# Causal mask of a 16-head attention: by TensorE into PSUM, or by VectorE on negated scores

## The chip, the cores and the metric

The program runs on one core of one Trainium2 chip. The core has a matrix engine (TensorE), two engines for elementwise work on 128 partitions (VectorE and ScalarE), a programmable one (GpSimd), and SyncE, which issues most transfers. Each engine runs its own instructions in order, and they wait for one another through semaphores. TensorE writes to PSUM, the accumulator memory; VectorE and ScalarE read PSUM and SBUF, GpSimd only SBUF. The metric is the device time of one execution in microseconds, and lower is better.

## The reference

Eight layers work on a state `x` of 32 sequences of 128 tokens of width 128, all float32: attention, linear experts, wide attention, capacity experts, attention with selection, GELU experts, attention, quantised convolution. Only the third, the wide attention, is touched. Cut to what matters it is

```python
# q = layernorm(x), k = v = ctx_1024; 16 heads of width 64; w_q, w_k, w_v are 1024 x 128
qh = (q @ w_q.T).reshape(b, n, H, D_K).transpose(0, 2, 1, 3)      # kh, vh likewise
scores = jnp.einsum('bhid,bhjd->bhij', qh, kh) / math.sqrt(D_K)
causal = jnp.tril(jnp.ones((n, n), dtype=bool))
scores = jnp.where(causal[None, None], scores, -jnp.inf)
attn = jax.nn.softmax(scores, axis=-1)
out = jnp.einsum('bhij,bhjd->bhid', attn, vh)
out = out.transpose(0, 2, 1, 3).reshape(b, n, H * D_V)
x = x + jnp.tanh(g_xattn[1]) * (out @ w_o.T)
```

So each query may look at keys up to its own place, and the others get probability 0.

## The kernel before

`program` keeps `x` in SBUF for the whole run and calls the stages one after another, each in a block of its own, so that a stage starts when every engine is through with the one before it. `setup` writes constants: among them, by GpSimd, `causal` (0 up to the diagonal and -1e30 above it, 128x128 in bf16) and `causal_swapped`, the same table with its halves of 64 rows exchanged.

`attention_wide` (from L2106) goes over 64 steps n. A step is one sequence and one octet of heads: 8 heads, so that 2 steps make a sequence and 4 steps a group of two sequences. `scores[n % 2]` is a PSUM tile of 1024 columns, two halves h of 4 heads (c) by 128 keys. Within a step:

- TensorE, `score(n)` (L2217): four bf16 matmuls of 64 rows by 64 columns of the array and 512 moving columns write the mask into the two halves (L2227). They use the four quadrants of the array, one each. Then 8 float32 matmuls of 64 rows add q times k on top of it (L2232); the trace has two records for each float32 matmul.
- VectorE, `maximum(n)` (L2375): one reduction over the 1024 columns gives 8 negated maxima.
- ScalarE, `exponents(n, h)` (L2315): four exponentials of 128 columns for each half, with the negated maximum as bias, and the row sums beside them. q was scaled as it was copied out of PSUM (L2304).
- VectorE, `invert(n, h)` (L2383): reciprocals of the four row sums of a half.
- GpSimd (L2183): the probabilities of a half times these reciprocals, in SBUF.
- TensorE, `turn(n)` (L2264): 16 transposes of 64 columns put the probabilities back into `scores[n % 2]`, turned. The second half waits for GpSimd's second product.
- VectorE, `copy_turned(n, h)` (L2368): two copies of 512 columns to SBUF. `score(n + 2)` waits for both.
- TensorE, `contexts(n)` (L2238), ScalarE, `context_copy(n)` (L2308), TensorE, `project_out(n)` (L2252): probabilities times v, their copy, and the output product. VectorE then adds the result to `x` once for each sequence (L2394) and takes its statistics (L2399).

The inputs of the next group are made between these by TensorE, `make(f)` (L2191): 13 tiles for each group, x, k0 to k3, q0 to q3, v0 to v3, into two PSUM buffers in turn. `make(f)` waits until tile f - 2 has been copied out. x and the q's are copied by ScalarE, the k's and v's by VectorE (`keep`, L2353). The 13 tiles are dealt to the four steps of a group: four, three, three and three (`quarter`, L2140).

The order on each engine is written out by hand. TensorE, in step n: the first two tiles of the step, `score(n + 1)`, `turn(n)`, `contexts(n - 1)`, the other tiles, `project_out(n - 1)`. ScalarE: copies of the first two tiles, `context_copy(n - 1)`, `exponents(n + 1, 0)`, the other copies, `exponents(n + 1, 1)`. VectorE (L2401 to L2419): copy of the first tile, `invert(n, 1)`, copy of the second tile, in every second step the addition to `x` and its statistics, in every fourth the normalisation of the next group, then `maximum(n + 1)`, `copy_turned(n, 0)`, `copy_turned(n, 1)`, copies of the other tiles, `invert(n + 1, 0)`.

`Chain` (L77) is a helper: an instruction that it is called with raises a semaphore, and the engine waits for it before it goes on.

Of the kernel before, what the change touches and what calls it, by code (L numbers as in the profile page):

```python
# [203 lines left out]
def setup(nc, st, arg):  # L204


    with ExitStack() as ctx:
# [3 lines left out]
        w_zero, swapped = sem("w_zero"), sem("swapped")  # L211
# [13 lines left out]
        def _(pool):  # L225
# [5 lines left out]
            nc.gpsimd.memset(st.causal[:, :], 0.0)  # L231
            nc.gpsimd.memset(st.causal_swapped[:, :], 0.0)
# [14 lines left out]
            nc.gpsimd.affine_select(out=st.causal[:, :], in_=st.causal[:, :], compare_op=ALU.is_ge, fill=NEVER,  # L247
# [6 lines left out]
            nc.gpsimd.memset(st.ones_b[:, :], 1.0).then_inc(swapped, 1)  # L254
            for half in range(2):
                pool.wait_ge(swapped, half + 1)
                if half == 0:
                    nc.gpsimd.memset(heads_apart(st.v_pad, 0, 1), 1.0)
                    nc.gpsimd.memset(heads_apart(st.v_pad, 1, 1), 1.0)
                rows = slice(half * 64, half * 64 + 64)  # L260
                nc.gpsimd.affine_select(out=st.causal_swapped[rows, :], in_=st.causal_swapped[rows, :], compare_op=ALU.is_ge,
                                        fill=NEVER, base=64 - 64 * half, pattern=[[-1, P]], channel_multiplier=1).then_inc(swapped, 1)
# [1843 lines left out]
def attention_wide(nc, st, arg):  # L2106
# [3 lines left out]
    with ExitStack() as ctx:  # L2110
# [6 lines left out]
        def sem(n):  # L2117
# [7 lines left out]
        heads_t = sb("heads_t", [P, 2, CH * S])  # L2125
        scores = [ps("scores0", 2 * CH * S), ps("scores1", 2 * CH * S)]
# [3 lines left out]
                 "heads_done acc_done x_done").split()  # L2130
# [56 lines left out]
        def _(pe):  # L2187
# [29 lines left out]
            def score(n):  # L2217
# [7 lines left out]
                for h, table in enumerate((st.causal, st.causal_swapped)):  # L2225
                    for r in range(2):
                        nc.tensor.matmul(scores[n % 2][rows((r + h) % 2), h * 512:h * 512 + 512], st.identb[rows(r), rows(r)],  # L2227
                                         table[rows(r), :].unsqueeze(1).to_broadcast([DKW, CH, S]), start=True, stop=False,
                                         skip_group_check=True)
                for c in range(CH):  # L2230
                    for h in range(2):
                        last = nc.tensor.matmul(scores[n % 2][:, h * 512 + c * S:h * 512 + (c + 1) * S],  # L2232
                                                q_t[rows(h), group % 2, CH * o + c, u * S:(u + 1) * S],
                                                k_t[rows(h), group % 2, CH * o + c, u * S:(u + 1) * S],
                                                start=False, stop=(c == CH - 1), skip_group_check=True)
# [53 lines left out]
        def _(act):  # L2289
            ln_scalar(act)  # L2290

            def keep(f):
# [9 lines left out]
                else:  # L2302
                    wait(act, s["s_done"], 4 * (group - 1))
                    last = nc.scalar.activation(q_t[:, group % 2, 2 * part:2 * part + 2, :].rearrange("p c q -> p (c q)"),  # L2304
                                                made[f % 2][:, :], ACT.Copy, scale=scale)
# [9 lines left out]
            def exponents(n, h):  # L2315
                if not real(n):
                    return
                act.wait_ge(s["max_done"], n + 1)
                wait(act, s["t_done"], 2 * (n - 2) + h + 1)
                for c in range(CH):  # L2320
                    i = CH * h + c
                    last = nc.scalar.activation(probs[:, n % 2, h, c * S:(c + 1) * S],  # L2322
                                                scores[n % 2][:, i * S:(i + 1) * S], ACT.Exp,
# [14 lines left out]
        def _(dve):  # L2338
# [36 lines left out]
            def maximum(n):  # L2375
                if not real(n):
                    return
                dve.wait_ge(s["s_done"], n + 1)
                wait(dve, s["exp_done"], 2 * (n - 2) + 2)
                v.tensor_reduce(neg_max[:, n % 2, :], scores[n % 2][:, :].rearrange("p (h k) -> p h k", k=S),  # L2380
                                axis=X_AXIS, op=ALU.max, negate=True).then_inc(s["max_done"], 1)
# [18 lines left out]

            normalise(0)  # L2401
# [155 lines left out]
def program(nc, arg, out, stages=8):  # L2557
    st = Persistent()
    with ExitStack() as ctx:
# [8 lines left out]
        st.row0, st.causal, st.causal_swapped = (sb(n, [P, P], BF16) for n in ("row0", "causal", "causal_swapped"))  # L2568
# [89 lines left out]
```

## Time and profile before

| | |
|---|---|
| time, median of 3 runs (lowest to highest) | 1752.95 us (1750.25 to 1754.14) |
| the profiled execution's own time, its span | 1754.32 us, 1752.6 us |
| TensorE matmul, busy over the span | 1585.0 us, 90% |
| VectorE, ScalarE, GpSimd, busy over the span | 61%, 53%, 32% |
| wide attention (from the exponentials' table to the last copy of the heads) | 321.5 to 762.9 us |
| the mask matmuls (L2227), in the whole run | 256 matmuls, 0.40 us each, four side by side |
| maximum (L2380) | 64 times 1222 ns |
| exponentials (L2322) | 512 times 386 ns, their sums' read 228 ns |
| probabilities turned, copied out (L2373) | 128 times 681 ns |

The span is the profiled execution as the hardware profiler saw it, and its own time stands beside it because the medians come from other executions. Busy shares are averages over eight stages with different limits. A matmul's end is modelled, so that a busy TensorE need not be one at its peak. Rows of the timeline give the start, the duration, and the engine, line and operation; "x16" are records merged in one row, whose duration is that of the whole row; a bracket gives the idle time ahead of it and who ended it. In rows of windows each engine has its busy time, with its count of records behind it, in the order PE, PEld, DVE, ACT, POOL; then come the granted clock as a share of 2.4 GHz, the DMA share and GB/s.

### The profile page before, as it was taken

What the parts mean: (1) busy time and instruction counts of PE and PEld (TensorE: products, weight loads), DVE (VectorE), ACT (ScalarE), POOL (GpSimd) and SP (SyncE); (2) the same over time, 40 slices, a digit from 0 to 9 for tenths busy, and PEclk for the clock granted to TensorE, in tenths of its full rate; (3) what the DMA queues carried; (4) which work ended last, traced back from release to release, by engine and by line L of the source; (5) the groups of instructions that cost most, each with busy time, mean ns of one, the idle gap of its engine ahead of it and who ended that gap; (6) DMA issues with size and microseconds to landing.
All of it is one profiled execution on the core that took longest, in us unless ns stands there. A gap on an engine that the chain in (4) does not pass through costs nothing. (4 is left out here: it accounts for less than half of the span.)

```text
span 1752.6 us, 46417 instructions
## 1 busy us (share of the span) xinstructions
PE 1585.0 (90%) x17384; PEld 1060.8 (61%) x17384; DVE 1076.5 (61%) x2320; ACT 934.1 (53%) x2341; POOL 569.0 (32%) x1033
## 2 busy tenths in 40 slices
PE   4988799899999999987987799979999988898898
PEld 2555454677777777765775456647777754555354
DVE  5677767566666666645166788962322236777676
ACT  3777536455555656533444466634343337775354
POOL 3565319223233332310221345300000005654672
PEclk8999899999999999989999799979999989999899
DMA  7544130000000000010103344110000016541000
GB/s 182 142 130 128 42 107 0 10 8 7 5 8 4 8 8 4 2 49 5 44 1 84 108 110 112 37 37 0 1 0 0 0 50 158 143 124 61 8 19 25
DMA packets 114001, 86.40 MB, mean 49 GB/s; under 512 B 19344, under 2 KB 110736, under 8 KB 113808
## 3 DMA queue, kind: packets, MB, share of 16 engines
q1 hardware_dynamic: 106592, 81.30, 16.8%
q10 hardware_dynamic: 7216, 2.45, 0.8%
q8 instruction: 131, 2.15, 0.5%
q14 instruction: 62, 0.51, 0.1%
HBM read 22.88 MB, written 2.10 MB: 14 GB/s over the span
## 5 line engine op out<-in xcount | busy, mean ns | idle before, releaser
L1090 DVE TENSOR_REDUCE neg_max<-scores 128x8 f32<-128x1024 f32 x192 | 233.1, 1215 | 80.6 <-PE scores L715 34.1
L2183 POOL TENSOR_TENSOR probs<-probs,inverse 128x512 f32<-128x512 f32 x128 | 133.0, 1039 | 314.3 <-DVE inverse L2388 314.2
L2322 ACT ACTIVATE probs<-scores,neg_max 128x128 f32<-128x128 f32 x512 | 180.2, 386 | 5.3 <-DVE neg_max L2380 5.3
L959 ACT ACTIVATE probs<-turned 128x1024 bf16<-128x1024 f32 (+1 forms) x128 | 130.9, 1023 | 86.2 <-PE turned L738 86.1
L1841 ACT ACTIVATE hidden_f<-hb_f,b_f 128x512 f32<-128x512 f32 x128 | 87.8, 687 | 129.0 <-PE hb_f L1787 128.7
L546 POOL TENSOR_TENSOR k_all<-k_all,k_parts 128x512 f32<-128x512 f32 x24 | 27.8, 1157 | 325.7 <-ACT k_parts L885 325.7
L1796 PEld LDWEIGHTS yb_f<-w_f,hidden_f 128*128 128x128 f32 x1024 | 119.2, 192 | 14.8 <-issue 14.8
L2313 ACT ACTIVATE heads_t<-heads 128x512 f32<-128x512 f32 x64 | 38.2, 598 | 165.8 <-PE heads L2248 165.8
L1796 PE MATMUL yb_f<-w_f,hidden_f 128*128 128x128 f32 x1024 | 119.3, 275 | 0.0
L1787 PE MATMUL hb_f<-xn_all_f,w_f 128*128 (+1 forms) x256 | 116.8, 600 | 0.0
L2322 ACT ACTIVATION_READ_ACCUMULATOR probs<-scores,neg_max 128x1 f32 x512 | 116.6, 228 | 0.0
L1866 DVE TENSOR_TENSOR y_sum_f<-yb_f,b_f 128x512 f32<-128x512 f32 x32 | 22.1, 692 | 150.4 <-PE yb_f L1796 150.4
L2380 DVE TENSOR_REDUCE neg_max<-scores 128x8 f32<-128x1024 f32 x64 | 78.2, 1222 | 35.4 <-PE scores L2232 35.4
L566 POOL CAST spread<-neg_max 128x16 bf16<-128x16 f32 x96 | 26.7, 278 | 211.2 <-issue 194.3
L959 ACT ACTIVATE probs<-turned,key_cols 128x1024 f32<-128x1024 f32 x64 | 71.2, 1113 | 34.6 <-PE turned L738 34.3
L1986 PE MATMUL conv_f<-conv_weights_or_copies,xq_t_f 128*128 128x512 f32 x192 | 87.9, 593 | 0.3 <-ACT xq_t_f L2022 0.3
L764 PE MATMUL heads<-probs,v_pad 128*32 128x128 f32 x2048 | 85.4, 286 | 0.3 <-ACT probs L959 0.2
L2373 DVE COPY probs_t<-scores 128x512 f32<-128x512 f32 x128 | 81.9, 681 | 2.2 <-PE scores L2273 2.2
L2260 PEld LDWEIGHTS y_ps<-y_weights_or_value_parts,heads_t 128*128 128x128 f32 x512 | 68.3, 195 | 21.0 <-ACT heads_t L2313 19.0
L738 PE MATMUL turned<-shift,ones_b 32*128 32x512 bf16 x384 | 77.3, 399 | 0.7
L1787 PEld LDWEIGHTS hb_f<-xn_all_f,w_f 128*128 128x128 f32 x256 | 46.9, 193 | 47.5 <-issue 47.5
L2232 PE MATMUL scores<-k_t,q_t 64*128 64x128 f32 x1024 | 74.4, 285 | 0.0
(342 smaller groups left out, 3768.1 us busy)
## 6 DMA issues: line engine op xcount, KB each, us to landing
k_rep<-k_parts SPq DMA_DIRECT2D x144, 128.0 KB, 2.5
q_rep<-q_parts SPq DMA_DIRECT2D x129, 128.0 KB, 2.5
dense<-both SPq DMA_DIRECT2D x120, 64.0 KB, 2.1
ctx_t<-in_ctx_t_dram SPq DMA_DIRECT2D x24, 256.0 KB, 4.0
conv_weights_or_copies<-k_parts SPq DMA_DIRECT2D x32, 128.0 KB, 2.5
conv_weights_or_copies<-q_parts SPq DMA_DIRECT2D x32, 128.0 KB, 2.5
w_f<-in_L_ffn_W_dram SPq DMA_DIRECT2D x16, 256.0 KB, 3.2
x_state<-in_x_dram SPq DMA_DIRECT2D x4, 512.0 KB, 8.1
```

The source lines that it names most:

```text
L738: last = nc.tensor.matmul(turned[:, (g % 2) * 512:(g % 2 + 1) * 512], ones_b[quad_rows(g), :], shift[quad_rows(g), b % 2, :], start=False, ...
L764: last = nc.tensor.matmul(heads[b % 2][32 * j:32 * j + 32, half * S:half * S + S], v_pad[:, b % 2, first + 32 * j:first + 32 * j + 32], pr ...
L959: nc.scalar.activation(probs[:, b % 2, pair, :], turned[:, :], ACT.Exp, **bias).then_inc(s["exp_done"], 1)
L1090: v.tensor_reduce(neg_max[:, b % 2, 8 * pair:8 * pair + 8], scores[pair][:, :].rearrange("p (h k) -> p h k", k=S), axis=X_AXIS, op=ALU.max ...
L1787: nc.tensor.matmul(hb[c][:, :], w1[:, e, c * P:(c + 1) * P], cols(xn_all, k, BT), start=True, stop=True).then_inc(h_done, 1)
L1796: last = nc.tensor.matmul(yb[e % 2][:, j * D:(j + 1) * D], hidden[:, e % 2, c, j * S:(j + 1) * S], w2[:, e, c, :], start=(c == 0), stop=(c ...
L1841: nc.scalar.activation(hidden[:, e % 2, c, :], hb[c][:, :], ACT.Gelu, bias=b1[:, e * HC + c:e * HC + c + 1]) \
L1986: nc.tensor.matmul(conv[b % 2][:, :], xq_t[:, b % 2, k:k + S], w_tap[:, k, :], start=(k == 0), stop=False)
L2183: nc.gpsimd.tensor_tensor(p4, p4, inverse[:, n % 2, CH * h:CH * h + CH].unsqueeze(2).to_broadcast([P, CH, S]), ALU.mult).then_inc(s["prob_ ...
L2322: last = nc.scalar.activation(probs[:, n % 2, h, c * S:(c + 1) * S], scores[n % 2][:, i * S:(i + 1) * S], ACT.Exp, bias=neg_max[:, n % 2, ...
L2373: v.tensor_copy(probs_t[:, n % 2, h, :], scores[n % 2][:, h * 512:h * 512 + 512]).then_inc(s["pt_done"], 1)
L2380: v.tensor_reduce(neg_max[:, n % 2, :], scores[n % 2][:, :].rearrange("p (h k) -> p h k", k=S), axis=X_AXIS, op=ALU.max, negate=True).then ...
```

## The change

The mask leaves TensorE. q is copied with the opposite sign, so that `scores` holds the negated scores, and the first matmul of each half starts the accumulation. VectorE adds a table `future` (0 up to the diagonal, +1e30 above it, now 128x128 in float32, repeated for the four heads) to 512 columns of the negated scores, writes the sum to a new SBUF tile `masked`, waits for that, and takes the minimum over the keys of each head, which is the negated maximum. This is done for each half in turn, and each half raises `max_done` by one. ScalarE waits for its own half only and takes the exponential of minus `masked` plus the negated maximum. `setup` writes one table where it wrote two.

```diff
# setup, GpSimd
-            nc.gpsimd.memset(st.causal[:, :], 0.0)
-            nc.gpsimd.memset(st.causal_swapped[:, :], 0.0)
+            nc.gpsimd.memset(st.future[:, :], 0.0)
...
-            nc.gpsimd.affine_select(out=st.causal[:, :], in_=st.causal[:, :], compare_op=ALU.is_ge, fill=NEVER,
+            nc.gpsimd.affine_select(out=st.future[:, :], in_=st.future[:, :], compare_op=ALU.is_ge, fill=-NEVER,
                                     base=0, pattern=[[-1, P]], channel_multiplier=1).then_inc(consts, 1)
...
-                nc.gpsimd.affine_select(out=st.causal_swapped[rows, :], in_=st.causal_swapped[rows, :], compare_op=ALU.is_ge,
-                                        fill=NEVER, base=64 - 64 * half, pattern=[[-1, P]], channel_multiplier=1).then_inc(swapped, 1)
# attention_wide
+        masked = sb("masked", [P, 2, 2 * CH * S])
# TensorE, score(n)
-                for h, table in enumerate((st.causal, st.causal_swapped)):
-                    for r in range(2):
-                        nc.tensor.matmul(scores[n % 2][rows((r + h) % 2), h * 512:h * 512 + 512], st.identb[rows(r), rows(r)],
-                                         table[rows(r), :].unsqueeze(1).to_broadcast([DKW, CH, S]), start=True, stop=False,
-                                         skip_group_check=True)
                 for c in range(CH):
                     for h in range(2):
                         last = nc.tensor.matmul(scores[n % 2][:, h * 512 + c * S:h * 512 + (c + 1) * S],
...
-                                                start=False, stop=(c == CH - 1), skip_group_check=True)
+                                                start=(c == 0), stop=(c == CH - 1), skip_group_check=True)
# ScalarE, keep(f) for q, and exponents(n, h)
-                                                made[f % 2][:, :], ACT.Copy, scale=scale)
+                                                made[f % 2][:, :], ACT.Copy, scale=-scale)
...
-                act.wait_ge(s["max_done"], n + 1)
+                act.wait_ge(s["max_done"], 2 * n + h + 1)
...
-                                                scores[n % 2][:, i * S:(i + 1) * S], ACT.Exp,
+                                                masked[:, n % 2, i * S:(i + 1) * S], ACT.Exp, scale=-1.0,
                                                 bias=neg_max[:, n % 2, i:i + 1], accum_out=row_sum[:, n % 2, i:i + 1])
# VectorE, maximum(n); link = Chain(dve, s["chain"])
-                v.tensor_reduce(neg_max[:, n % 2, :], scores[n % 2][:, :].rearrange("p (h k) -> p h k", k=S),
-                                axis=X_AXIS, op=ALU.max, negate=True).then_inc(s["max_done"], 1)
+                for h in range(2):
+                    half = masked[:, n % 2, h * 512:h * 512 + 512].rearrange("p (c k) -> p c k", k=S)
+                    link(v.tensor_tensor(half, scores[n % 2][:, h * 512:h * 512 + 512].rearrange("p (c k) -> p c k", k=S),
+                                         st.future[:, :].unsqueeze(1).to_broadcast([P, CH, S]), ALU.add))
+                    v.tensor_reduce(neg_max[:, n % 2, CH * h:CH * h + CH], half, axis=X_AXIS, op=ALU.min).then_inc(s["max_done"], 1)
```

## Rows read from the trace of the kernel before

**Rows 1.** Busy time by engine in the whole wide-attention stage; PEclk is the granted clock

```profile
321.50:758.00 436.50, 425.49 (x4445) 328.50 (x4444) 279.67 (x536) 252.43 (x1163) 133.03 (x128) 1.00 0.02 6
```

**Rows 2.** VectorE, the same instruction of the first and the fifteenth step D

```profile
349.18 0.34 DVE L2394 SCALAR_TENSOR_TENSOR x_state<-y_ps,tanh_g,x_state 128x128 f32<-128x128 f32 x1
...
729.98 0.34 DVE L2394 SCALAR_TENSOR_TENSOR x_state<-y_ps,tanh_g,x_state 128x128 f32<-128x128 f32 x1
```

**Rows 3.** TensorE in order of time, steps D to C; start, duration, operation, [idle]

```profile
674.86 0.40 PE L2227 MATMUL scores<-causal,identb 64*64 64x512 bf16 x2
...
675.20 1.16 PE L2232 MATMUL scores<-k_t,q_t 64*128 64x128 f32 x16
...
676.78 1.09 PE L2248 MATMUL heads<-probs_t,v_sb 128*64 128x128 f32 x16
...
679.88 1.05 PE L2213 MATMUL made<-ctx_t,y_weights_or_value_parts 128*128 128x256 f32 x4
680.86 0.40 PE L2227 MATMUL scores<-causal,identb 64*64 64x512 bf16 x2
...
683.09 1.09 PE L2248 MATMUL heads<-probs_t,v_sb 128*64 128x128 f32 x16
...
686.83 1.03 PE L2213 MATMUL made<-ctx_t,y_weights_or_value_parts 128*128 128x256 f32 x4
...
690.58 1.09 PE L2248 MATMUL heads<-probs_t,v_sb 128*64 128x128 f32 x16
...
697.37 1.09 PE L2248 MATMUL heads<-probs_t,v_sb 128*64 128x128 f32 x16
```

**Rows 4.** VectorE in order of time, steps D and A

```profile
676.67 1.22 DVE L2380 TENSOR_REDUCE neg_max<-scores 128x8 f32<-128x1024 f32 x1
677.80 1.28 DVE L2373 COPY probs_t<-scores 128x512 f32<-128x512 f32 x2
679.00 0.68 DVE L2366 COPY v_sb<-made 128x512 f32<-128x512 f32 x1
...
681.34 0.18 DVE L2388 RECIPROCAL inverse<-row_sum 128x4 f32<-128x4 f32 x1 [1.22 <-ACT probs L2322]
```

**Rows 5.** ScalarE in order of time, step D

```profile
677.92 0.60 ACT L2313 ACTIVATE heads_t<-heads 128x512 f32<-128x512 f32 x1 [3.22 <-PE heads L2248]
678.42 0.36 ACT L2322 ACTIVATE probs<-scores,neg_max 128x128 f32<-128x128 f32 x1
```

**Rows 6.** GpSimd in order of time, step A

```profile
681.60 1.04 POOL L2183 TENSOR_TENSOR probs<-probs,inverse 128x512 f32<-128x512 f32 x1 [0.35 <-DVE inverse L2388]
```

**Rows 7.** VectorE and TensorE where group 1 is filled, at the stage's head

```profile
326.28 0.68 DVE L2366 COPY v_sb<-made 128x512 f32<-128x512 f32 x1
...
327.11 1.10 PE L2213 MATMUL made<-ctx_t,y_weights_or_value_parts 128*128 128x256 f32 x4 [0.74 <-DVE v_sb L2366]
```

**Rows 8.** Groups of instructions over the whole kernel: busy us, mean ns | idle before

```profile
L1866 DVE TENSOR_TENSOR y_sum_f<-yb_f,b_f 128x512 f32<-128x512 f32 x32 | 22.1, 692 | 150.4 <-PE yb_f L1796 150.4
...
L2058 DVE TENSOR_REDUCE amax_f<-xn_all_f 128x4 f32<-128x512 f32 x7 | 4.7, 677 | 0.9 <-POOL xn_all_f L1925 0.9
...
L1067 DVE TENSOR_TENSOR q_all<-q_all,q_parts 128x512 f32<-128x512 f32 x4 | 3.7, 936 | 11.2 <-ACT q_parts L885 11.2
...
L885 ACT ACTIVATE k_parts<-k_all 128x512 bf16<-128x512 f32 x24 | 15.0, 623 | 0.3
```

**Rows 9.** VectorE in the last stage, a linked pair of instructions

```profile
1641.24 0.69 DVE L2070 TENSOR_REDUCE hmax_f<-act_h_f 128x1 f32<-128x512 f32 x1 [1.37 <-ACT act_h_f L2027]
1641.96 0.15 DVE L2071 TENSOR_SCALAR hmax_f<-hmax_f 128x1 f32<-128x1 f32 x1
```

**Rows 10.** GpSimd and VectorE in the setup, their last instructions

```profile
8.61 0.72 POOL L261 TENSOR_SCALAR_AFFINE_SELECT causal_swapped<-causal_swapped 64x128 bf16<-64x128 bf16 x2
...
13.87 0.35 DVE L279 TENSOR_REDUCE ident<-ident 128x32 f32<-128x128 f32 x1
```

**Rows 11.** Busy time by engine behind the last step of the stage

```profile
760.00:766.00 6.00, 4.34 (x26) 3.42 (x25) 0.65 (x2) 0.60 (x1) 0.00 (x0) 0.50 0.00 0
```

More of the change, by code:

```diff
@@ L210, in setup @@
         x_in, g_in, zeroed, consts = [sem(f"x_in{c}") for c in range(4)], sem("g_in"), sem("zeroed"), sem("consts")
-        w_zero, swapped = sem("w_zero"), sem("swapped")
+        w_zero, padded = sem("w_zero"), sem("padded")
         block = ctx.enter_context(nc.Block())
@@ L253, in _ @@
             nc.gpsimd.memset(st.spread[:, :, :], 0.0)
[L254 to L260, printed above, removed]
-                nc.gpsimd.affine_select(out=st.causal_swapped[rows, :], in_=st.causal_swapped[rows, :], compare_op=ALU.is_ge,
-                                        fill=NEVER, base=64 - 64 * half, pattern=[[-1, P]], channel_multiplier=1).then_inc(swapped, 1)
+            nc.gpsimd.memset(st.ones_b[:, :], 1.0).then_inc(padded, 1)
+            pool.wait_ge(padded, 1)
+            nc.gpsimd.memset(heads_apart(st.v_pad, 0, 1), 1.0)
+            nc.gpsimd.memset(heads_apart(st.v_pad, 1, 1), 1.0)
         @block.scalar
@@ L2129, in attention_wide @@
         names = ("xn_done made_done act_kept dve_kept s_done max_done exp_done inv_done prob_done t_done pt_done pv_done "
-                 "heads_done acc_done x_done").split()
+                 "heads_done acc_done x_done chain").split()
         s = {n: sem(n) for n in names}
@@ L2399, in statistics @@
                 v.bn_stats(cols(st.stats, b, 6), cols(st.x, b, D))
+            link = Chain(dve, s["chain"])
             normalise(0)
@@ L2567, in program @@
         st.ones, st.tri = sb("ones", [P, P]), sb("tri", [P, P])
-        st.row0, st.causal, st.causal_swapped = (sb(n, [P, P], BF16) for n in ("row0", "causal", "causal_swapped"))
+        st.row0, st.future = sb("row0", [P, P], BF16), sb("future", [P, P])
         st.ident32 = sb("ident32", [P, 32])
```

## The prediction

> **What bounds the kernel now.** Only one stage is touched, so I first read what the engines do in it. From 321.5 to 758 us TensorE is busy for 425.5 of 436.5 us, while VectorE is busy for 280, ScalarE for 252, GpSimd for 133, and TensorE's granted clock is 1.00 throughout [rows 1]. The plain reading is that TensorE bounds the stage and VectorE has a third of its time free. Such a share does not say where the waits end, so I then read one group of four steps in order of time.
>
> I call the four kinds of step by what they make: A (x, k0, k1, k2), B (k3, q0, q1), C (q2, q3, v0), D (v1, v2, v3). The same instruction of step D comes at 349.18 and, 14 groups on, at 729.98: 380.8 / 14 = 27.20 us for a group [rows 2]. Start of `contexts` to start of `contexts` (L2248), the four steps take D to A 683.09 - 676.78 = 6.31, A to B 7.49, B to C 6.79, and C to D what is left, 27.20 - 20.59 = 6.61 [rows 3]. These have two different limits.
>
> The first is a loop through all four engines. It runs contexts, copy of the heads, 8 exponentials, reciprocal, GpSimd's product, second half of the transposes, next contexts. From the rows: 676.78 to the first exponential 678.42 is 1.64, from there to the second reciprocal 681.34 is 2.92, GpSimd starts at 681.60 (+0.26) and needs 1.04, and contexts start 683.09 - 682.64 = 0.45 later [rows 3 to 6]. Sum 6.31: D to A is this loop. B to C is the loop too: ScalarE there copies q1 between the two halves of the exponentials, and the 0.48 by which 6.79 exceeds 6.31 is such a copy (the heads' copy holds ScalarE for 678.42 - 677.92 = 0.50) [rows 5].
>
> The second limit is TensorE's own work, in A to B and C to D. Only there can TensorE's saving appear.
>
> A third limit is one step from acting. `make(k0)` in step A writes the PSUM buffer that VectorE empties by the copy of v3, and that copy stands behind `maximum` and two `copy_turned` in VectorE's order. At the stage's head, where this wait does show, v3's copy starts at 326.28 and k0 at 327.11: 0.83 from the one to the other, with TensorE idle for 0.74 [rows 7]. In the steady group v3's copy starts at 679.00 and k0 at 679.88 [rows 3, 4]. So 0.05 us is all the slack there is. VectorE is 64% busy and yet cannot be late there.
>
> **What is removed.** The four mask matmuls run side by side, from 674.86 to the scores at 675.20: 0.34 us a step, and 64 steps make 21.8 us if all of it reached the end [rows 3]. It reaches it in A to B (7.15 then) and C to D (6.27), not in the two loop-bound intervals.
>
> **What VectorE gets.** Before: one maximum of 1024 columns, 1.13 us start to start (676.67 to 677.80) [rows 4]. After, per half: an addition with one operand in PSUM, then a minimum read from SBUF. The nearest rows have the very shapes: an addition 128x512 with a PSUM operand lasts 692 ns, a reduction 128x512 to 4 from SBUF 677 ns [rows 8]. A linked instruction starts 0.03 behind its forerunner's end (1641.24 + 0.69, next 1641.96) [rows 9], so the addition takes 0.72. Unlinked ones overlap by 0.08 (two copies take 1.20, each lasting 0.68) [rows 4], so the minimum takes 0.60. T = 2 x (0.72 + 0.60) = 2.64, I use 2.65: 1.52 more than before. Bounds: T = 2.4 if the link costs nothing, and 3.1 if the addition took the 936 ns of an addition with both operands in SBUF [rows 8]. I stay at 2.65 since only one operand is in SBUF here.
>
> **What ScalarE gets.** The exponentials now read SBUF. No row has this form from SBUF. Copies of 512 columns take 0.60 us from PSUM [rows 5] and 0.623 from SBUF [rows 8]: 0.023 each, 0.2 for 8, and the loop becomes 6.51. Bounds: 0, and 0.35 as below. That the first half may start after its own minimum changes nothing: that is ready 1.41 + 0.05 after the first addition starts, and ScalarE is held by the heads' copy until about the same moment, 678.42 - 676.67 = 1.75 in step D [rows 4, 5].
>
> On this term the Trainium skill speaks against the change. "VectorE: DVE Perf Modes", section "The TRN2 errata — SBUF-src ops pay a fixed extra latency per instruction", gives ScalarE 224 cycles of fixed cost from SBUF and 172 from PSUM. By that, an estimate from this page, 52 cycles at 1.2 GHz are 0.043 us each and 0.35 a step; two intervals a group would lengthen by 0.14 more, some 4 us in all. It also gives VectorE a smaller fixed cost from SBUF (58 against 120 cycles), which the trace does not bear out: 677 ns for the reduction from SBUF, 680 for a copy from PSUM [rows 4, 8]. I therefore let the rows decide.
>
> **The group walked through**, zero at the start of the scores in step D. (Before, `maximum` starts 1.47 later; the mask was 0.34 of what went ahead, and VectorE's work ahead of it is timed by the v's, so 1.81 now.)
> D to A: copies at 1.81 + 2.65 = 4.46, v3's copy at 4.46 + 1.20 = 5.66, k0 at 5.66 + 0.83 = 6.49, scores 0.98 later (679.88 to 680.86) at 7.47, contexts 1.58 behind the scores (675.20 to 676.78) at 9.05 [rows 3]. Contexts of D itself are at 1.83 (below), so TensorE alone would have started k0 679.88 - 676.78 = 3.10 later, at 4.93: it stands idle for 1.6 us. The loop's side is as late: the first reciprocal comes behind v3's copy at 6.26, GpSimd at 6.52, both halves by 8.60, contexts at 9.05. So D to A = 9.05 - 1.83 = 7.22.
> A to B: scores of A at 7.47, so the additions start at 7.47 + 1.16 + 0.05 = 8.68, k1's copy at 8.68 + 2.65 + 1.20 = 12.53, k3 at 13.36. TensorE alone would be there 686.83 - 683.09 = 3.74 behind contexts, at 12.79: wait 0.57. A to B = 7.15 + 0.57 = 7.72.
> B to C: loop with q1, 6.79 + 0.20 = 6.99. In B and C VectorE has nothing between its copies and the reciprocal but v0, and stays off the path.
> C to D: TensorE needs 6.27, the loop 6.51. So 6.5, and contexts of D come 0.24 later against the scores: 1.58 + 0.25 = 1.83, as used.
> Sum 7.22 + 7.72 + 6.99 + 6.50 = 28.43, against 27.20: +1.23 a group, although TensorE does 1.36 less. VectorE itself stays below its limit: 17.4 us a group before (280 / 16) and 6.1 more.
>
> **The sum.** 15 groups from the first step D to the last: 15 x 1.23 = 18.5. The first k0, in the head, is later too: 1.2 once. Behind the last step D, the loop with nothing to fill: the late reciprocal once, 1.2, and 4 steps x 0.2 = 0.8. Setup: GpSimd drops one memset and two selections, the last of which start at 8.61, while VectorE's last instruction there starts at 13.87, behind the loads of x, which do not change: 0 [rows 10]. If that cover were gone it would be the 0.7 us of those selections. Total +21.7. The profiled execution took 1754.32 (span 1752.6), so it would take 1776.0; the median of the three runs shown is 1752.95, 1.4 lower, and there it is 1774.7. **Forecast 1775 us.**
>
> **Range of this case.** T at 2.4 takes 0.25 from D to A and 0.25 from A to B: -7.5. Exponentials as fast as from PSUM take 0.4 off a group: -6, together about 1761. T at 3.1 gives +13 or so, 1789.
>
> **The rivals.**
> (1) Faster, TensorE's saving reaches the end because VectorE's extra work falls into its idle time. For it: VectorE idles 27.2 - 17.4 = 9.8 us a group and is given 6.1. The place that decides is v3's copy ahead of k0: D to A is T + 4.57, so it falls back to the loop's 6.31 only if T is below 1.75 (1.5 where the exponentials are no slower, since contexts of D then stand at 1.6). The group would then be 6.31 + 7.15 + 6.79 + 6.31 = 26.56, -0.64 x 15 = -10, 1743 us, and that only with exponentials no slower. Against it: two pairs of instructions of 512 columns cannot be brought below 2.4 by any row. 9%.
> (2) No change, within 3.5 us of 1753: the same places, with T near 2 and exponentials as before. 6%.
> (3) Much slower: the addition and GpSimd's product disturb each other at SBUF, T = 3.1 and the product late in the loop, +1 us a group more, or the stage's tail loses its clock. Behind the last step of this stage the granted clock is 0.50, the 1.2 GHz level, after steps in which TensorE mostly waited [rows 11], and it has 0.34 less to do there now; a tail step at that level puts half the transposes and the contexts, 0.4 + 1.1 us, on the loop once more. Together 1791 and above. For it: 936 against 692 ns by operand place [rows 8]. Against: the addition has one SBUF operand, and GpSimd works mostly while VectorE waits. 12%.
> (4) Forecast, 1761 to 1791: 70%; 3% for slower by less, 1757 to 1761.
>
> **How the numbers follow.** Slower by over 0.2% (3.5 us, about what a measurement of this kernel tells from no change): 70 + 12 + 3 = 85%. Same 6%, faster 9%. The range 1760 to 1792 holds case 4 and the lower part of 3, and leaves out 1 and 2.
>
> **What would show each step.** A group's period of 28.4 (right), 27.2 or less (wrong). TensorE idle about 1.6 us ahead of k0 in L2213's rows, released by VectorE's copy of v_sb, 15 or 16 times, and some 0.5 us ahead of k3, released by k_t. The additions at 0.69 and minima at 0.68, starts 0.72 and 0.60 apart. ScalarE's exponentials some 0.025 further apart than 0.34. B to C at 7.0. The forecast is wrong if k0 does not wait, or if GpSimd's product or the additions come out far from 1.04 and 0.69.

## The result, and the profile after

The changed kernel takes 1773.2 us (median of 4 runs, 1769.9 to 1775.5) against 1751.6 us before: a ratio of 1.0128, 95% interval 1.0109 to 1.0147, or 22 us more. The profiled execution was the fastest of the four, with a span of 1768.1 us.

The stage itself went from 457.5 us to 481.2 (from the square root of its layer norm, L306 before and L300 after, to that of the next stage): +23.7. The whole span grew by 15.5 only (1752.6 to 1768.1): in this pair of profiles the stages that the change does not touch were together 8.2 us shorter. Between the profiles of all kernels here one such stage moved by up to 5 us against the kernel before, so comparisons below go by the group's period and the ratio of runs, not by spans. First the stage as a whole, the columns being those of [rows 1]:

```profile
321.50:773.00 451.50, 410.02 (x4132) 320.70 (x4131) 357.74 (x716) 266.13 (x1150) 130.55 (x126) 0.99 0.02 6
```

TensorE is busy for 410 us instead of 425, and VectorE for 358 instead of 280. TensorE is thus no longer busy all the time: 410 of 451.5.

TensorE in order of time, from step A over B and C to D and A again; these answer to [rows 3]:

```profile
642.52 1.09 PE L2238 MATMUL heads<-probs_t,v_sb 128*64 128x128 f32 x16
...
646.73 1.13 PE L2208 MATMUL made<-ctx_t,y_weights_or_value_parts 128*128 128x256 f32 x4 [0.30 <-DVE k_t L2356]
...
650.24 1.09 PE L2238 MATMUL heads<-probs_t,v_sb 128*64 128x128 f32 x16
...
657.31 1.09 PE L2238 MATMUL heads<-probs_t,v_sb 128*64 128x128 f32 x16
...
662.00 1.16 PE L2222 MATMUL scores<-k_t,q_t 64*128 64x128 f32 x16
...
663.90 1.09 PE L2238 MATMUL heads<-probs_t,v_sb 128*64 128x128 f32 x16
...
668.60 1.10 PE L2208 MATMUL made<-ctx_t,y_weights_or_value_parts 128*128 128x256 f32 x4 [1.44 <-DVE v_sb L2356]
669.63 1.16 PE L2222 MATMUL scores<-k_t,q_t 64*128 64x128 f32 x16
...
671.21 0.98 PE L2238 MATMUL heads<-probs_t,v_sb 128*64 128x128 f32 x14
```

Start to start of the contexts: A to B 7.72, B to C 7.07, C to D 6.59, D to A 7.31. The group takes 28.69 us instead of 27.20, for 14 groups on end (349.18 to 729.98 in [rows 2], now 347.25 to 748.91). Ahead of k0 at 668.60 TensorE stands idle for 1.44 us, released by VectorE's copy of v3; ahead of k3 at 646.73 for 0.30, released by the copy of k1.

VectorE in the same step D, as [rows 4]:

```profile
663.93 0.68 DVE L2372 TENSOR_TENSOR masked<-scores,future 128x512 f32<-128x512 f32 x1
664.65 0.69 DVE L2374 TENSOR_REDUCE neg_max<-masked 128x4 f32<-128x512 f32 x1
665.25 0.68 DVE L2372 TENSOR_TENSOR masked<-scores,future 128x512 f32<-128x512 f32 x1
665.97 0.69 DVE L2374 TENSOR_REDUCE neg_max<-masked 128x4 f32<-128x512 f32 x1
666.57 1.28 DVE L2363 COPY probs_t<-scores 128x512 f32<-128x512 f32 x2
667.77 0.68 DVE L2356 COPY v_sb<-made 128x512 f32<-128x512 f32 x1
668.37 0.17 DVE L2381 RECIPROCAL inverse<-row_sum 128x4 f32<-128x4 f32 x1
```

Addition to minimum 0.72, minimum to addition 0.60, and 2.64 from the first addition (663.93) to the copies (666.57). v3's copy starts at 667.77 and k0 0.83 later. ScalarE in this step, as [rows 5]:

```profile
665.04 0.60 ACT L2303 ACTIVATE heads_t<-heads 128x512 f32<-128x512 f32 x1 [2.92 <-PE heads L2238]
665.53 0.39 ACT L2312 ACTIVATE probs<-masked,neg_max 128x128 f32<-128x128 f32 x1
...
665.92 0.39 ACT L2312 ACTIVATE probs<-masked,neg_max 128x128 f32<-128x128 f32 x1
```

The exponentials are 0.385 apart, where they were 0.343. The groups of the stage's instructions (busy us, mean ns, then idle before them) put the two costs side by side:

```profile
L2312 ACT ACTIVATE probs<-masked,neg_max 128x128 f32<-128x128 f32 x512 | 197.4, 390 | 5.8 <-DVE neg_max L2374 5.8
...
L2312 ACT ACTIVATION_READ_ACCUMULATOR probs<-masked,neg_max 128x1 f32 x511 | 97.0, 190 | 0.0
L2374 DVE TENSOR_REDUCE neg_max<-masked 128x4 f32<-128x512 f32 x128 | 87.9, 686 | 4.4
L2372 DVE TENSOR_TENSOR masked<-scores,future 128x512 f32<-128x512 f32 x127 | 87.0, 685 | 25.5 <-PE scores L2222 25.5
...
L2208 PE MATMUL made<-ctx_t,y_weights_or_value_parts 128*128 128x256 f32 x240 | 63.4, 397 | 28.4 <-DVE v_sb L2356 22.3 <-DVE k_t L2356 6.0
```

The exponential is hardly longer than the 386 ns of before. What overlaps less is only seen in the starts. The k tiles' matmuls (L2208) carry 28.4 us of idle time, 22.3 of it behind v3's copy and 6.0 behind k1's.

### The profile page after: what moved, and what is told of

Read it like the earlier page. It is cut to its first block and busy times, and to the rows that moved or that the text cites. A ratio compares the mean times of both kernels' runs of the same rounds, so it can differ in the third digit from the quotient of the medians.

```text
span 1768.1 us, 46092 instructions
## 1 busy us (share of the span) xinstructions
PE 1566.6 (89%) x17128; PEld 1051.8 (59%) x17128; DVE 1158.6 (66%) x2512; ACT 952.2 (54%) x2341; POOL 569.2 (32%) x1030
## 5 line engine op out<-in xcount | busy, mean ns | idle before, releaser
L1084 DVE TENSOR_REDUCE neg_max<-scores 128x8 f32<-128x1024 f32 x192 | 233.0, 1214 | 77.7 <-PE scores L709 33.1
L2312 ACT ACTIVATE probs<-masked,neg_max 128x128 f32<-128x128 f32 x512 | 197.4, 390 | 5.8 <-DVE neg_max L2374 5.8
L953 ACT ACTIVATE probs<-turned 128x1024 bf16<-128x1024 f32 (+1 forms) x128 | 131.0, 1024 | 82.7 <-PE turned L732 82.5
L2372 DVE TENSOR_TENSOR masked<-scores,future 128x512 f32<-128x512 f32 x128 | 87.7, 685 | 25.5 <-PE scores L2222 25.5
L2312 ACT ACTIVATION_READ_ACCUMULATOR probs<-masked,neg_max 128x1 f32 x512 | 97.2, 190 | 0.0
L2208 PE MATMUL made<-ctx_t,y_weights_or_value_parts 128*128 128x256 f32 x256 | 67.2, 396 | 28.4 <-DVE v_sb L2356 22.3
L2374 DVE TENSOR_REDUCE neg_max<-masked 128x4 f32<-128x512 f32 x128 | 87.9, 686 | 4.4
L2222 PEld LDWEIGHTS scores<-k_t,q_t 64*128 64x128 f32 x1024 | 63.0, 189 | 28.1 <-DVE v_sb L2356 12.1
```

What stands on the lines that cost most here:

```text
L953: nc.scalar.activation(probs[:, b % 2, pair, :], turned[:, :], ACT.Exp, **bias).then_inc(s["exp_done"], 1)
L1084: v.tensor_reduce(neg_max[:, b % 2, 8 * pair:8 * pair + 8], scores[pair][:, :].rearrange("p (h k) -> p h k", k=S), axis=X_AXIS, op=ALU.max ...
L2372: link(v.tensor_tensor(half, scores[n % 2][:, h * 512:h * 512 + 512].rearrange("p (c k) -> p c k", k=S), st.future[:, :].unsqueeze(1).to_b ...
L2374: v.tensor_reduce(neg_max[:, n % 2, CH * h:CH * h + CH], half, axis=X_AXIS, op=ALU.min).then_inc(s["max_done"], 1)
```

## The experiments

All kernels of a table row are compared with the kernel before on the same chip. "D to A" and so on are start to start of the contexts in the profile, in one group in the middle of the stage.

| kernel | D to A | A to B | B to C | C to D | group | ratio to before, 95% interval |
|---|---|---|---|---|---|---|
| before | 6.31 | 7.49 | 6.79 | 6.61 | 27.20 | 1 |
| changed | 7.31 | 7.72 | 7.07 | 6.59 | 28.69 | 1.0128 (1.0109 to 1.0147) |
| e1, no mask at all | 6.31 | 7.15 | 6.79 | 6.31 | 26.56 | 0.9925 (0.9897 to 0.9953) |
| e2, exponentials from PSUM | 7.50 | 7.71 | 6.80 | 6.37 | 28.38 | 1.0089 (1.0064 to 1.0115) |
| e3, k and v copies first | 7.07 | 7.59 | 7.07 | 6.72 | 28.45 | 1.0101 (1.0077 to 1.0124) |
| e4, and the reciprocal | 6.58 | 7.26 | 7.07 | 6.72 | 27.63 | 1.0048 (1.0028 to 1.0067) |
| e5, masked scores in PSUM | 7.53 | 7.74 | 6.79 | 6.39 | 28.45 | 1.0129 (1.0110 to 1.0148) |
| e6, e5 with e4's order | 6.30 | 7.25 | 6.79 | 6.72 | 27.06 | 1.0001 (0.9984 to 1.0018) |
| e7, one addition of 1024 | 7.57 | 7.15 | 7.65 | 6.59 | 28.96 | 1.0167 (1.0141 to 1.0192) |
| e8, before with e4's order | 6.60 | 7.49 | 6.80 | 6.72 | 27.61 | 1.0038 (1.0023 to 1.0052) |
| e9, e6 with the order in D and A only | 6.56 | 7.25 | 6.80 | 6.40 | 27.01 | 1.0002 (0.9992 to 1.0012) |
| e10, e9 with v2 on ScalarE | 6.31 | 7.25 | 6.79 | 6.40 | 26.75 | 0.9987 (0.9970 to 1.0005) |
| e11, changed with v2 on ScalarE | 7.09 | 7.72 | 7.07 | 6.58 | 28.46 | 1.0123 (1.0096 to 1.0150) |
| e12, before with v2 on ScalarE | 6.30 | 7.49 | 6.79 | 6.62 | 27.20 | 1.0000 (0.9983 to 1.0017) |

### e1: what TensorE's saving is worth

```diff
# the kernel before, score(n)
-                for h, table in enumerate((st.causal, st.causal_swapped)):
-                    for r in range(2):
-                        nc.tensor.matmul(... table ...)
-                                                start=False, ...
+                                                start=(c == 0), ...
```

> The kernel before with the four mask matmuls of each step taken out and nothing in their place (the causal mask is left out altogether). What TensorE's saving is worth alone. Theory 1 (two intervals of a group are bound by the loop through four engines, two by TensorE): D to A 6.31, A to B 7.15, B to C 6.79, C to D 6.31, group 26.56 instead of 27.20, some 10 us less, ratio to before 0.994. Rival (TensorE bounds all four): 0.34 in each of 64 steps, 21.8 us less, ratio 0.9875, group 25.8.

All four intervals came out to 0.01. Of TensorE's 1.36 us a group only 0.64 arrives: 0.34 in A to B and 0.30 in C to D, where the loop stops it. The median is 12.8 us lower, and the 10 expected lie within the ratio's interval. That TensorE bounds every step is refuted.

### e2: the exponentials' source

```diff
# the changed kernel, exponents(n, h)
-                                                masked[:, n % 2, i * S:(i + 1) * S], ACT.Exp, scale=-1.0,
+                                                scores[n % 2][:, i * S:(i + 1) * S], ACT.Exp, scale=-1.0,
```

> The changed kernel, but the exponentials read the negated scores in PSUM instead of the masked ones in SBUF (the mask is left out of the exponentials; VectorE's work is unchanged). Theory 1 (VectorE's order is most of the loss, the exponentials' source a part): exponentials 0.343 apart again instead of 0.385, B to C 6.8, C to D 6.3, while D to A stays at 7.3 to 7.4 and A to B at 7.7, since VectorE sets them; group about 28.25 instead of 28.69, some 6 us less than the changed kernel, ratio to before 1.009. Rival 2 (the exponentials' source is the main loss): group 27.3 or less, ratio 1.001.

B to C falls to the loop's old length (6.80) and C to D nearly so (6.37, where e1 has 6.31); D to A rises from 7.31 to 7.50, and A to B stays at 7.71. TensorE's rows in D to A show why:

```profile
662.06 1.09 PE L2238 MATMUL heads<-probs_t,v_sb 128*64 128x128 f32 x16
...
666.95 1.10 PE L2208 MATMUL made<-ctx_t,y_weights_or_value_parts 128*128 128x256 f32 x4 [1.63 <-DVE v_sb L2356]
...
669.56 1.09 PE L2238 MATMUL heads<-probs_t,v_sb 128*64 128x128 f32 x16
```

k0's wait is 1.63 us, 0.2 longer than in the changed kernel, since the contexts of D now come earlier and VectorE does not. The source in SBUF costs 0.31 a group (28.69 to 28.38), VectorE's work the rest.

### e3 and e4: VectorE's order

```diff
# the changed kernel, VectorE; e3 without the lines on invert, e4 with them
                 maximum(n + 1)
+                for f in todo[2:]:
+                    keep(f)
+                if n % 4 in (0, 3):
+                    invert(n + 1, 0)
                 copy_turned(n, 0)
                 copy_turned(n, 1)
-                for f in todo[2:]:
-                    keep(f)
-                invert(n + 1, 0)
+                if n % 4 in (1, 2):
+                    invert(n + 1, 0)
```

> The changed kernel with VectorE's copies of v3, k1, k2 and v0 put ahead of the two copies of the turned probabilities; the first reciprocal stays last. Theory 1: k0 no longer waits 1.4 us for v3's copy, but the first reciprocal is as late as it was, and with it GpSimd and the transposes, so D to A stays near 7.3 with the wait moved to the transposes; A to B loses its 0.4 us ahead of k3 and goes to about 7.2. Group 28.2, some 7 us less than the changed kernel, ratio to before 1.008. Rival (only the PSUM buffer counts): D to A falls to 6.6 too, group 27.5, ratio 1.003.

> As the one with the copies first, and in steps D and A the first reciprocal too stands ahead of the copies of the turned probabilities. Theory 1: both ways on which VectorE was late are open, D to A falls to the loop with the slower exponentials, 6.6; A to B 7.2, B to C 7.1, C to D 6.6: group 27.4 to 27.5, some 18 us less than the changed kernel, ratio to before about 1.002. Rival 3 (VectorE is simply too busy, 23.5 of 27 us): group stays at 28 or above, the lateness shows elsewhere, ratio 1.007 or more.

With the copies first (e3), no wait ahead of k0 or k3 is left in the trace, and D to A is still 7.07. The wait has moved to GpSimd's product, ahead of the second half of the transposes:

```profile
661.84 1.09 PE L2238 MATMUL heads<-probs_t,v_sb 128*64 128x128 f32 x16
...
668.51 0.46 PE L2263 MATMUL scores<-ident,probs 64*128 64x64 f32 x8 [0.45 <-POOL probs L2178]
668.90 1.09 PE L2238 MATMUL heads<-probs_t,v_sb 128*64 128x128 f32 x16
```

A to B missed its forecast: 7.59 instead of 7.2, although k3 no longer waits. In step A too the first reciprocal stood last, so that GpSimd's two products ran end to end and the transposes waited for the second.

With the reciprocal moved as well (e4), D to A falls to 6.58 and the ratio from 1.0128 to 1.0048, some 14 us of the 22. In D to A the copies alone brought 0.24 us, the reciprocal on top of them 0.49 more. The reciprocal moved alone was not run, so what it would bring by itself is not shown.

e4's group is 27.63 for the 27.4 to 27.5 expected, and 0.12 of this is in C to D (6.72 for 6.6). There v0's copy stands ahead of the turned copies and is itself not ready, as e6 shows below; the first reciprocal comes later, and the transposes wait for GpSimd. In D to A the scores wait 0.35 us for the turned copies that now come later, but D to A is still as short as the loop.

```profile
645.62 1.09 PE L2238 MATMUL heads<-probs_t,v_sb 128*64 128x128 f32 x16
...
651.95 0.46 PE L2263 MATMUL scores<-ident,probs 64*128 64x64 f32 x8 [0.23 <-POOL probs L2178]
...
652.34 1.09 PE L2238 MATMUL heads<-probs_t,v_sb 128*64 128x128 f32 x16
...
657.16 1.16 PE L2222 MATMUL scores<-k_t,q_t 64*128 64x128 f32 x16 [0.35 <-DVE probs_t L2363]
...
658.93 1.09 PE L2238 MATMUL heads<-probs_t,v_sb 128*64 128x128 f32 x16
```

### e5 and e6: masked scores in PSUM

```diff
# the changed kernel, maximum(n) and exponents(n, h); e6 has e4's order as well
-                    half = masked[:, n % 2, h * 512:h * 512 + 512].rearrange("p (c k) -> p c k", k=S)
+                    half = scores[n % 2][:, h * 512:h * 512 + 512].rearrange("p (c k) -> p c k", k=S)
-                                                masked[:, n % 2, i * S:(i + 1) * S], ACT.Exp, scale=-1.0,
+                                                scores[n % 2][:, i * S:(i + 1) * S], ACT.Exp, scale=-1.0,
```

> The changed kernel with the masked negated scores written back to where they were in PSUM: the additions write PSUM, the minima and the exponentials read it. The whole result is computed. Theory 1: exponentials 0.343 apart, additions and minima as long as before (0.69 and 0.68; no run has shown an addition that writes PSUM, between 0.6 and 0.8), so as with the exponentials from PSUM: D to A 7.5, A to B 7.7, B to C 6.8, C to D 6.35, group 28.4, ratio to before 1.009. Rival 2 (a PSUM operand more makes VectorE slower): additions above 0.8, group 28.8 or more, ratio 1.013 or more.

> Masked scores in PSUM, and VectorE's copies of v3, k1, k2, v0 ahead of the copies of the turned probabilities, in steps D and A the first reciprocal as well. Theory 1: all that was lost is found, and TensorE's 0.34 shows where TensorE bounds: D to A 6.35, A to B 7.2, B to C 6.8, C to D 6.4, group 26.7 to 26.8, 7 us less than before, ratio 0.996, and so below both kernels. Rival 3 (VectorE too busy): group 27.3 or more, ratio 1.000 or above.

An addition that writes PSUM costs no more than one that writes SBUF, as its group in e5 shows:

```profile
L2372 DVE TENSOR_TENSOR scores<-scores,future 128x512 f32<-128x512 f32 x127 | 88.1, 693 | 27.1 <-PE scores L2222 27.1
```

e5's group is e2's within 0.07. Its runs, however, are those of the changed kernel (1.0129 against e2's 1.0089); the stage took 477.2 us in e5's profile and 477.0 in e2's, so this difference of the ratios does not show in the stage. The two were measured on different chips, and their intervals just touch (1.0110 to 1.0148, 1.0064 to 1.0115); I leave it open.

e6 ends level with the kernel before rather than below it. D to A, A to B and B to C came as expected, C to D did not (6.72 for 6.4). VectorE in step C there:

```profile
642.33 0.69 DVE L2374 TENSOR_REDUCE neg_max<-scores 128x4 f32<-128x512 f32 x1
643.30 0.69 DVE L2356 COPY v_sb<-made 128x512 f32<-128x512 f32 x1 [0.28 <-PE made L2202]
643.91 1.28 DVE L2363 COPY probs_t<-scores 128x512 f32<-128x512 f32 x2
645.11 0.17 DVE L2381 RECIPROCAL inverse<-row_sum 128x4 f32<-128x4 f32 x1
```

v0 is not made yet when its copy's turn comes: VectorE waits 0.28, the copies go after it, and the first reciprocal starts at 645.11, after which the second half of the transposes waits for GpSimd. The order costs e3 and e4 the same 0.13 in C to D (6.72 for the changed kernel's 6.59).

### e7: one addition instead of two

```diff
# the changed kernel, maximum(n)
-                for h in range(2):
-                    ... an addition and a minimum of 512 columns, max_done + 1
+                both = masked[:, n % 2, :].rearrange("p (c k) -> p c k", k=S)
+                link(v.tensor_tensor(both, scores[n % 2][:, :].rearrange("p (c k) -> p c k", k=S),
+                                     st.future[:, :].unsqueeze(1).to_broadcast([P, 2 * CH, S]), ALU.add))
+                v.tensor_reduce(neg_max[:, n % 2, :], both, axis=X_AXIS, op=ALU.min).then_inc(s["max_done"], 2)
```

> The changed kernel with one addition of 1024 columns and one minimum of 1024 in place of two of each: T is 1.25 + 1.15 = 2.4 rather than 2.64, but no half is ready before 2.5 us from the start of the addition instead of 1.45. Theory 1 with ScalarE's start as a second condition: k0 comes 0.25 earlier but the exponentials now wait for the minimum in D, A and B, by 0.5 to 0.9 us, so D to A 7.5, A to B 7.5, B to C 7.6, C to D 6.6, group 29.2, ratio to before 1.017. Rival 4 (only VectorE's total time counts): the group falls by 0.5 to 28.2, ratio 1.008.

VectorE needs less time for the mask (1.32 + 1.14 = 2.46 us, from the first start to the copies, for 2.64), and the kernel is slower. ScalarE and VectorE in step D:

```profile
641.55 0.60 ACT L2303 ACTIVATE heads_t<-heads 128x512 f32<-128x512 f32 x1 [2.92 <-PE heads L2238]
643.01 0.40 ACT L2312 ACTIVATE probs<-masked,neg_max 128x128 f32<-128x128 f32 x1 [0.87 <-DVE neg_max L2373]
...
640.44 1.22 DVE L2371 TENSOR_TENSOR masked<-scores,future 128x1024 f32<-128x1024 f32 x1
641.76 1.22 DVE L2373 TENSOR_REDUCE neg_max<-masked 128x8 f32<-128x1024 f32 x1
```

ScalarE is through with the heads' copy and waits 0.87 us for the minima. A to B came out better than expected (7.15 for 7.5) and the rest came within 0.07. The halves of the change are worth 0.3 us a group.

### e8 and e12: controls on the kernel before

```diff
# e8: the kernel before with e4's order (as above)
# e12: the kernel before, v2 kept by ScalarE
-        kept_by = ["act" if kind in "xq" else "dve" for kind, _ in order]
+        kept_by = ["act" if kind in "xq" or (kind, part) == ("v", 2) else "dve" for kind, part in order]
```

> A control: the kernel before, mask matmuls and all, with the same order of VectorE's copies and reciprocals as in the run with both put first. Theory 1: before, VectorE is not late anywhere, so nothing is gained; v0's copy ahead in step C cost 0.13 in C to D in the other runs and may do so here. Group 27.2 to 27.35, ratio 1.000 to 1.002. Rival: the order itself is better whatever the mask does, group 26.9 or less, ratio below 0.997.

> Control: the kernel before with v2 copied by ScalarE. Before, D to A is the loop and VectorE is not late, so theory 1 says no change: group 27.20, ratio 0.999 to 1.001. Rival: the copy on ScalarE is a gain of its own, ratio 0.998 or less.

e8 missed: the new order is not neutral before, it costs 0.41 us a group. Its one wait of TensorE there is for the copies it puts off:

```profile
656.77 0.40 PE L2227 MATMUL scores<-causal,identb 64*64 64x512 bf16 x2 [0.55 <-DVE probs_t L2373]
```

So what e4 and e6 gain is not a better order in itself: it paid only where VectorE was late, and in the kernel before it cost 0.3 us in D to A and 0.1 in C to D. e12 changed nothing (27.20 and 1.0000).

### e9, e10 and e11: the rest of VectorE's lateness

```diff
# e9: e6, with
+                early = n % 4 in (0, 3)    # copies and reciprocal ahead of the turned copies in D and A alone
# e10: e9 with v2 kept by ScalarE; e11: the changed kernel with v2 kept by ScalarE and nothing else
```

> As the run with masked scores in PSUM and the new order, but the new order in steps D and A only; in C, v0's copy stands behind the copies of the turned probabilities again (there VectorE had waited 0.28 us for v0 and was then late with the first reciprocal, and C to D was 6.72). Theory 1: C to D falls to 6.35 or 6.4, the others stay at 6.31, 7.25, 6.79: group 26.75 rather than 27.07 and 27.20, 15 groups make 6.5 to 7 us less than before, ratio 0.996, faster than both kernels. Rival: the new order in D makes the scores wait for the turned copies whatever C does, C to D stays at 6.7, ratio 1.000.

> As the run with masked scores in PSUM and the new order in D and A, and v2 is copied out of PSUM by ScalarE, which idles 3 us there, instead of VectorE. In that run D to A was 6.56, since the additions of step D began 0.6 behind the end of the scores' latency, held by v2's copy, and k0 still waited 0.46. Theory 1: the additions begin 0.6 earlier, D to A falls to the loop's 6.31; A to B 7.2, B to C 6.8, C to D 6.35 to 6.4: group 26.7 to 26.75, ratio to before 0.996. Rival 3 (VectorE too busy, something else of it is late instead): D to A 6.5 or more, ratio 1.000.

> The changed kernel with one edit, v2 copied by ScalarE: only the start of step D's additions moves, by 0.6. Theory 1: D to A 7.31 - 0.6 = 6.7, the others as they were (7.7, 7.1, 6.6), group 28.1, some 9 us less than the changed kernel, ratio to before 1.008. Rival: D to A is set by something that does not depend on when VectorE begins, no change, ratio 1.0128.

e9: C to D fell to 6.40 as expected, but D to A rose from 6.31 to 6.56, for which k0's wait had been gone in e6 and is back:

```profile
647.38 1.10 PE L2208 MATMUL made<-ctx_t,y_weights_or_value_parts 128*128 128x256 f32 x4 [0.46 <-DVE v_sb L2356]
```

What C no longer loses, D does. k0 starts 5.3 us behind D's scores in both kernels, set by VectorE (651.14 - 645.80 in e6, 647.38 - 642.08 in e9), while D's own contexts now come 0.45 us earlier against those scores. e10 takes v2 from VectorE and reaches the group forecast, 26.75, with k0 no longer waiting:

```profile
672.16 1.09 PE L2238 MATMUL heads<-probs_t,v_sb 128*64 128x128 f32 x16
...
675.41 1.10 PE L2208 MATMUL made<-ctx_t,y_weights_or_value_parts 128*128 128x256 f32 x4
676.84 1.16 PE L2222 MATMUL scores<-k_t,q_t 64*128 64x128 f32 x16 [0.32 <-DVE probs_t L2367]
...
678.46 1.09 PE L2238 MATMUL heads<-probs_t,v_sb 128*64 128x128 f32 x16
```

Its ratio missed, 0.9987 for the 0.996 expected: the best estimate is a gain of 2 us, the interval (0.9970 to 1.0005) goes from 5 us less to 1 us more, and so the gain is not told from none. Of the 0.45 us a group, 6 us in 14 groups, the stage's whole length shows 3.7 (457.5 to 453.8); the tail took most of the rest (see the clock below). No version that computes the whole result is clearly faster than the kernel before.

e11 missed its size and held the mechanism. The additions should have begun 0.6 us earlier and began 0.22 earlier (661.51 - 659.80 = 1.71 behind the scores' start, 1.93 in the changed kernel); D to A fell by just that, 7.31 to 7.09. This stands in the trace alone: the ratios of e11 and the changed kernel, 1.0123 and 1.0128, are not told apart. VectorE, GpSimd and TensorE there:

```profile
660.04 0.32 DVE L2391 SCALAR_TENSOR_TENSOR x_state<-y_ps,tanh_g,x_state 128x128 f32<-128x128 f32 x1
660.40 0.30 DVE L2396 BATCH_NORM_STATS2 ln_stats<-x_state 128x6 f32<-128x128 f32 x1
660.61 0.98 DVE L2343 TENSOR_SCALAR xn<-x_state,ln_mean,ln_rstd 128x128 f32<-128x128 f32 x2
661.51 0.68 DVE L2376 TENSOR_TENSOR masked<-scores,future 128x512 f32<-128x512 f32 x1
...
660.21 1.04 POOL L2178 TENSOR_TENSOR probs<-probs,inverse 128x512 f32<-128x512 f32 x1 [0.37 <-DVE inverse L2385]
...
666.17 1.10 PE L2208 MATMUL made<-ctx_t,y_weights_or_value_parts 128*128 128x256 f32 x4 [1.21 <-DVE v_sb L2360]
```

The two normalisations took 0.98 us instead of 0.59. The first began inside GpSimd's product (660.21 to 661.25) and lasted 0.72, ending 0.08 behind the product. It was so in 14 groups of e11, and in e12 and e10 as well (0.72 and 0.76 long, ending 0.08 behind the product); in the changed kernel it began only as the product ended, and lasted 0.33. That accounts for the 0.4 that the additions did not gain.

## Why the prediction was right, point by point

**The third limit.** v3's copy with its 0.05 us of slack was the step on which it all hung, and it was shown by runs: TensorE idle 1.4 us ahead of k0, 15 times. Against its contexts k0 came 668.60 - 663.90 = 4.70 us later instead of 3.10, and these are the 1.6 of the forecast. D to A was 7.31 (7.22); in e11 the start of the additions moved 0.22 and D to A with it. That the loop's side is equally late was a statement of the walk, and e3 against e4 bears it out: 0.24 us from the one, 0.49 more from both. A to B came out at 7.72 as forecast, but not quite by the forecast wait: k3 came 646.73 - 642.52 = 4.21 behind contexts for 3.74 before, 0.47 late for the 0.57 of the walk. The other 0.10 lies between k3 and the scores (1.92 for 1.82), where the walk had nothing, so that the exact hit is in part luck.

**TensorE's saving.** Forecast at 0.34 in A to B, 0.30 in C to D and nothing elsewhere; e1 gave exactly these.

**VectorE's price.** T, from the first addition to the turned copies, was forecast at 2.65 and measured at 2.64, with 0.72 and 0.60 inside it (addition to minimum, minimum to addition). The link costs 0.12 against an unlinked neighbour, as read from [rows 9] and [rows 4].

**ScalarE's price was too low.** I took 0.023 us for an operand in SBUF, from copies of 512 columns. The exponentials' starts are 0.042 further apart, so the second reciprocal comes 662.15 - 658.95 = 3.20 behind the first exponential instead of 2.92. It shows in B to C, 7.07 for 6.99, and C to D, 6.59 for 6.50, and by v2's copy behind that reciprocal in D to A, 7.31 for 7.22: it comes 1.00 behind v1's copy where it came 0.86, and the additions start 1.93 behind the scores for the 1.81 of the walk. This is the one place where the page that spoke against the change was nearer than my row: the Trainium skill, "VectorE: DVE Perf Modes", section on the TRN2 errata, has 52 cycles more from SBUF for ScalarE, 0.043 us by its 1.2 GHz, and by that rule, the trace agrees with 0.042. For VectorE the same section's smaller cost from SBUF did not appear: the minimum from SBUF lasts 686 ns, from PSUM in e5 and e6 692.

**The sum.** Forecast for the stage: 14 x 1.23 = 17.2, 2.4 ahead of these groups (one more group and the first k0), 2.0 behind them, 21.7 in all. Measured in the profiles: 14 x 1.49 = 20.9, 2.0 ahead (39.58 for 37.57 from the stage's square root) and 0.9 behind (39.97 for 39.10 to the next stage's), 23.7. The term that was mis-sized is the group, 1.23 for 1.49, and its cause is ScalarE's price above. By the medians the change cost 21.6, so that the forecast of 1775 against 1773.2 is closer than its terms are. That is luck of some 2 us. The untouched stages scatter by more than this between the profiles, and no run shows that they owe anything to the change.

**The clock in the tail.** This part of rival 3 came true, at a lower price than it had. Two windows of the tail, columns as in [rows 1]:

```profile
755.00:761.00 6.00, 4.20 (x56) 3.47 (x56) 3.92 (x7) 3.21 (x16) 1.99 (x3) 1.00 0.01 3
761.00:767.00 6.00, 3.92 (x38) 3.32 (x39) 4.47 (x9) 2.39 (x11) 1.30 (x2) 0.71 0.00 0
```

Before, the granted clock stayed at 1.00, 2.4 GHz, up to 755 us at least, two steps from the end. Now, after 6 us in which TensorE was busy for 4.2, it is 0.71 in the mean of 761 to 767 us, four steps from the end: part of that window is at the lower level, 1.2 GHz, and the output product there takes 2.08 us for 1.16. One step then lasts 7.28 us (757.79 to 765.07, copy of the heads to copy of the heads) for 6.30. The five such intervals behind the last D came to 32.8 us for 30.0. Rival 3 put 1.5 us a step on this; 7.28 is 0.7 above the changed kernel's loop, and the other slow step, 7.47, is 0.9 above it. Its reading that TensorE mostly waited before the clock fell in the kernel before holds only for the last 4 us ahead of the fall (busy for 1.5 of 753 to 757): from 735 to 753 us it was busy for 4.2 to 4.3 us in each 6, at a granted clock of 1.00.

Most of the 2.8 comes back at once. From the last copy of the heads to the next stage's square root it is now 5.0 us for 6.8: the granted clock is 1.00 there (784.1 to 787 us) where it was 0.50, the last output product takes 1.16 us for 2.08, and one short VectorE instruction of the next layer norm takes 0.18 for 1.03. The 0.9 us behind the groups is what is left. The forecast's 2.0 there held neither the slow steps nor this gain.

Such slow tail steps, one or two of 7.3 to 8.0 us, stand in the profile of every kernel here but the one before and e12, whose longest is 6.6. In e6, e9 and e10 the five intervals take 32.5, 32.5 and 32.8 us against 30.0: the groups of these kernels gained 2.0, 2.7 and 6.3 us, and 2.5 to 2.8 of it went there. There is one profile of each, and what decides when the clock falls is not shown: e8 keeps the mask matmuls and has a slow step too (7.41).

**The rivals.** That VectorE's idle time hides its extra work was refuted by e2 and e4: idle time it has (it still waits 38.5 us for ScalarE in the stage), but not ahead of v3's copy. No contention of the additions with GpSimd was seen: they keep 0.69 us throughout, and the products 1.04. The VectorE instruction that did wait for GpSimd is the normalisation, and only where an edit had moved it into the product (e10, e11, e12, and by 0.03 in e6).

**Shares.** From before to after, 27.20 to 28.69: -0.64 for the mask gone from TensorE (e1), +1.82 for VectorE's work (e2 against e1), +0.31 for the exponentials' source.

## What to carry to other kernels

The busy share of an engine says little on whether work may be added to it: look in its own order for the instruction behind which the bounding engine waits for a buffer, and measure the slack there. Here it was 0.05 us on an engine that idled a third of the time. When two ways are late together, undoing one shows little (0.24 of 0.73 us in step D to A), so they have to be opened together. And work taken from a bounding engine counts only in those steps where a loop through the others is not as long.

## What the runs showed of the hardware

- An operand's move from PSUM to SBUF shows in the distance of ScalarE's exponentials (0.343 to 0.385 us for 128 columns) and not in their duration (386 and 390 ns).
- VectorE's normalisation, float32 from SBUF to SBUF with 128 columns, takes 0.34 us. Where it began inside GpSimd's product in SBUF it ended 0.08 us behind the product's end, whenever it had begun: 0.72 us long in e11 and e12, 0.76 in e10, 0.37 in e6, in 14 groups each. The product kept its 1.04, and additions with one operand in PSUM kept 0.69.
- A linked addition of 512 columns holds the next instruction to 0.03 us behind its end, one of 1024 columns to 0.10 (641.76 - 640.44 - 1.22 in e7).
